# Slot tiles of the first expert layer: the h transposes ahead of the gathered rows' transpose on TensorE, with VectorE's two copies in the same order

## What is computed

```python
def _ffn(xn, rw, W1, W2):
    ms = jnp.mean(xn * xn, axis=-1, keepdims=True)
    h = xn * jax.lax.rsqrt(ms + RMS_EPS) * rw
    return jax.nn.silu(h @ W1) @ W2
...
gates = jax.nn.softmax(xf @ router_w, axis=-1)
top_v, top_i = jax.lax.top_k(gates, TOP_K)            # 2 of 14 experts
masked = jnp.zeros_like(gates).at[jnp.arange(N)[:, None], top_i].set(top_v)
masked = masked / (masked.sum(axis=-1, keepdims=True) + EPS)
routed_out = jnp.einsum('end,ne->nd', routed, masked)
return (routed_out + shared).reshape(B, T, D)         # 2 shared experts
```

## Time and profile before

| | us |
|---|---|
| runs of the kernel before | 988.82, 993.49, 994.43 (median 993.49) |
| the profiled execution, its own time | 996.92 |
| its span, first to last instruction | 995.2 |
| the slot loop in it: tile 0's gathered rows transposed to tile 44's output written | 367.1 to 445.7 |
| 40 of the 45 passes, first weight load of `slot_up` to the same 40 passes on | 377.35 to 441.56, 64.21 |

### The profile page before, as it was taken

How to read it: one execution, slowest core, us unless ns; L and a number is a source line. 1 busy time by engine, 2 the same in 40 slices (tenths; PEclk the granted TensorE clock), 3 DMA queues, 4 the chain that set the end, 5 groups by cost and what they waited for, 6 DMA issues and landing times.

```text
span 995.2 us, 18013 instructions
## 1 busy us (share of the span) xinstructions
PE 909.1 (91%) x5365; PEld 740.8 (74%) x5365; DVE 802.6 (81%) x2079; ACT 559.3 (56%) x1323; POOL 414.7 (42%) x480
## 2 busy tenths in 40 slices
PE   5999999999997898998878788988999999999995
PEld 5788888888884656765767676886667888888884
DVE  3778887888788955732898999986879999999996
ACT  2666666666667453444686433526775556655565
POOL 3566767576765425536540676642640000000001
PEclk7999999999998799999997999999999999999998
DMA  7232323333224103341102112001045666566651
GB/s 267 70 120 89 113 92 110 96 101 105 95 95 170 42 17 77 82 68 40 33 13 86 60 70 86 1 1 64 1 96 170 176 177 174 174 174 174 174 158 42
DMA packets 47122, 98.29 MB, mean 99 GB/s; under 512 B 7121, under 2 KB 23441, under 8 KB 45922
## 3 DMA queue, kind: packets, MB, share of 16 engines
q1 hardware_dynamic: 44610, 92.64, 30.2%
q0 software_dynamic: 2464, 5.05, 2.6%
HBM read 75.25 MB, written 22.41 MB: 98 GB/s over the span
## 4 chain that ended last, share of the span: by engine, by line
PE 66%; DVE 16%; issue 7%; ACT 5%; POOL 2%; DMA 1%; SPq 1%; another core or an unknown queue 0%; DVEq 0%; ACTq 0%; POOLq 0%
PE PS L1898 14%; PE PS L1899 13%; PE PS L1900 13%; PE PS L1965 4%; PE PS L1953 4%; PE PS L2144 3%; DVE rb L1695 2%; PE PS L1977 2%; PE PS L2158 2%; DVE P L1265 2%; PE PS L2087 1%; ACT P L903 1%; DVE keep L1676 1%; DVE xl L1235 1%; PE PS L2093 1%
## 5 line engine op out<-in xcount | busy, mean ns | idle before, releaser
L690 POOL TENSOR_TENSOR P<-P,rl 128x256 f32<-128x256 f32 (+1 forms) x130 | 104.9, 828 | 100.1 <-DVE rl L1272 100.1
L455 POOL TENSOR_TENSOR rs<-ms,neghalf 128x4 f32<-128x4 f32 (+1 forms) x28 | 26.0, 927 | 277.0 <-DVE nm L449 276.9
L1181 ACT ACTIVATE FG<-PS 128x512 f32<-128x512 f32 x112 | 67.1, 599 | 89.4 <-PE PS L1900 89.4
L903 ACT ACTIVATE P<-P,mn 128x128 f32<-128x128 f32 (+1 forms) x260 | 114.4, 444 | 3.1 <-DVE mn L1265 3.1
L1898 PE MATMUL PS<-XTh,W 128*128 128x512 f32 x256 | 100.5, 393 | 1.3 <-DMA W<-w3s 0.4
L1900 PE MATMUL PS<-XTh,W 128*128 128x512 f32 x256 | 99.7, 390 | 0.0
L1899 PE MATMUL PS<-XTl,W 128*128 128x512 f32 x256 | 99.7, 389 | 0.0
L1265 DVE CUSTOM_DVE_ANT_0 P<-PS,cmask 128x128 f32<-128x128 f32 (+1 forms) x260 | 77.1, 352 | 26.6 <-issue 26.6
L1864 DVE TENSOR_TENSOR FHL<-FH,FHH 128x512 fp32r<-128x512 f32 x128 | 90.0, 703 | 1.2 <-ACT FHH L1167 0.9
L1881 DVE TENSOR_TENSOR FU<-FG,PS 128x512 f32<-128x512 f32 x112 | 77.0, 687 | 16.1 <-ACT FG L1181 7.8
L911 ACT ACTIVATE Uh<-PS 128x512 fp32r<-128x512 f32 x64 | 38.4, 599 | 87.4 <-PE PS L1900 87.4
(11 more groups left out here) (479 smaller groups left out, 2609.2 us busy)
## 6 DMA issues: line engine op xcount, KB each, us to landing
GI<-coef SPq DMA_DIRECT2D x56, 256.0 KB, 4.2
GW<-coef SPq DMA_DIRECT2D x56, 256.0 KB, 4.1
w3s<-WS SPq DMA_DIRECT2D x32, 384.0 KB, 2.6
W<-w3s SPq DMA_DIRECT2D x32, 384.0 KB, 3.4
Wb<-decay SPq DMA_DIRECT2D x7, 1024.0 KB, 4.5
WR<-in_w SPq DMA_DIRECT2D x32, 192.0 KB, 2.5
WR<-in_w SPq DMA_DIRECT2D x16, 256.0 KB, 2.8
w12f<-WS SPq DMA_DIRECT2D x16, 256.0 KB, 2.0
```

Source lines behind the costliest of these rows:

```text
L690: last = pool.tensor_tensor(v, v, f, ALU.mult)
L903: last = act.activation(P[:, slot, c:c + w], P[:, slot, c:c + w], ACT.Exp, scale=-1.0, bias=mn[:, par, q:q + 1], accum_out=ls[:, par, q:q ...
L1181: act.activation(FG[:, k % 2, :], bank(4 + k % 2), ACT.Silu).then_inc(sem("fg_done"), 1)
```

## The change

On PE, `hidden_T(i-2)` is issued before `gather_T(i)` instead of after it. On DVE, the copy of `hTs` (with its waits) is issued before the copy of `xTs` (with its waits). No instruction is added or taken away, and no semaphore, buffer or shape changes. In the changed file the `hTs` copy has line 1533 and the `xTs` copy line 1538.

```diff
             for i in range(NT + 2):
+                if i >= 2:
+                    dve.wait_ge(sem("ht_ready"), on("ht_ready", i - 1))
+                    if i >= 4:
+                        dve.wait_ge(sem("yt_ready"), on("yt_ready", i - 3))
+                    dve.tensor_copy(hTs[i % 2][:, :], slot_hT).then_inc(sem("ht_done"), 1)
                 if i < NT:
                     dve.wait_ge(sem("xt_ready"), on("xt_ready", i + 1))
                     if i >= 2:
                         dve.wait_ge(sem("hs_ready"), on("hs_ready", i - 1))
                     dve.tensor_copy(xTs[i % 2][:, :], slot_xT).then_inc(sem("xt_done"), 1)
-                if i >= 2:
-                    dve.wait_ge(sem("ht_ready"), on("ht_ready", i - 1))
-                    if i >= 4:
-                        dve.wait_ge(sem("yt_ready"), on("yt_ready", i - 3))
-                    dve.tensor_copy(hTs[i % 2][:, :], slot_hT).then_inc(sem("ht_done"), 1)
...
             for i in range(NT + 3):
                 if 1 <= i < NT + 1:
                     slot_up(i - 1, experts[i - 1])
+                if 2 <= i < NT + 2:
+                    hidden_T(i - 2)
                 if i < NT:
                     gather_T(i)
-                if 2 <= i < NT + 2:
-                    hidden_T(i - 2)
```

## The result

| | before | changed |
|---|---|---|
| median of 8 runs, us | 993.22 (988.82 to 994.43) | 997.33 (996.9 to 1000.37) |
| 40 passes of the slot loop, us | 64.21 | 68.30 |
| one pass, median (shortest to longest), us | 1.54 (1.46 to 2.56) | 1.704 (1.70 to 1.80) |
| profiled execution, own time and span, us | 996.92, 995.2 | 997.02, 995.3 |

The changed kernel takes 1.0056 times as long, interval 1.0039 to 1.0073: slower by 4.1 us in the medians, where +5.0 was forecast. This ratio, like the others here, goes by the means of the runs (998.20 against 992.63, 5.6 us apart), and so it is a little larger than that of the medians. The 40 passes take 4.09 us more, where 4.2 was forecast.

A forecast was written before the change was run, and what follows sets the result against it. The prediction took PE's sequencer and matmuls to bound the slot loop, passing to a PE, VectorE, PE ring. Its terms 4.2 + 0.6 + 0.2 = +5.0 us took 993.5 to 998.5 us, range 993.0 to 1004.0.

The forecast's parts named there:

- The ring: Slot loop: PE, VectorE, PE hand-overs set the pace, 0.95 + 0.34 + 0.29 + 0.13 = 1.71 us a pass.
- T + 0.95, T + 1.29, T + 1.58: Slot loop, from `slot_up`'s weight load at T: `hTs` copy starts, `xTs` copy starts, `xTs` copy ends.
- Rival 4: VectorE in the slot loop: next copy waits for the previous one's end, 0.08 a pass, +3.4 us; chance 0.08.
- Rivals 1 to 3: Slot loop: `xTs` ready in time, 0 to 2 us, chance 0.2; a gain, 991.3, 0.05; late results compounding, 1002.5, 0.11.
- The cover: Slot loop: `xTs` is ready before PE's sequencer has its register, pass stays 1.55 to 1.60; chance 0.2.
- Late results: Slot loop: matmul results seen late, no longer paid for by slack, add 0.6 us, ends 0 and 2.
- a pass is set by PE's sequencer and matmuls: Slot loop before the change: other engines' results are ready earlier; a pass takes 1.605 us, 1.55 undisturbed.
- the wait is for the write of `Y` four tiles back: Two long passes before the change: `slot_down` waits for `Y`; the slower pace uses up most of this idle time.
- +4.2: Slot loop: 40 passes of 1.71 give 68.4 us against 64.2.
- First passes: Start of the slot loop: a pass of 1.35 becomes 1.71; counted as 0.2 us, ends 0 and 1.
- The stages before and behind the loop keep their lengths: Outside the slot loop: stage lengths unchanged, so a later loop end is passed on whole.
- PE's own row of work is as long as before.: PE in the slot loop: same matmuls and sequencer steps, so PE alone would keep its pass of 1.55.

The follow-up runs named there:

- e5: Changed kernel with two banks each for `slot_hT` and `slot_y`, no `ht_done` or `xt_done` waits on PE, looser `yt_done`: 1001.25 us, ratio 1.0056.
- e8: Changed kernel with only 128 of 256 columns of the `hTs` copy, output not the reference's: 991.06 us once, median pass 1.572.
- e3: Kernel before with only VectorE's copy order changed, TensorE's order kept: 1001.48 us, ratio 1.0134.
- e4: Kernel before without the redundant `xt_done` wait in `gather_T`: 987.97 us, ratio 0.9995.
- e7: Kernel before, own order kept, with the edits of e5: 993.28 us, ratio 0.9975.
- e10: Kernel before with eight `Y` buffers instead of four and nothing else: 994.15 us, ratio 0.9991.
- e9: e7 with eight `Y` buffers instead of four: 994.27 us, ratio 0.9991.
- e12: e9 without the gathers of tiles 4 to 44, output not the reference's: 980.46 us once, beside 992.0 for the kernel before.
- e11: Changed kernel run once more, no further edit: 998.7 us, ratio 1.0035.
- e2: Kernel before with only TensorE's order changed, VectorE's copy order kept: 993.02 us, ratio 1.0043.
- e6: The edit of e2 plus two `slot_hT` banks, `hidden_T` waiting for the copy of two tiles back: 994.37 us, ratio 0.9993.
- e1: Kernel before run again with a profile, no edit: 988.51 us, ratio 1.0001.

## Why the prediction was right, and where it wasn't

- **The ring.** T + 0.95, T + 1.29, T + 1.58 and a pass of 1.71 were forecast; 0.95, 1.29, 1.57 and 1.70 are in the trace. e5 shows that the waits for `Y` and for emptied banks don't hold the loop, e8 that the copy ahead counts fully, e3 that the same terms give 1.81 in the other order of transposes. The terms were read from single rows and added without averages: two hand-overs at which the receiving engine stood idle, VectorE's own distance from one copy to the next, and the length of a copy.
- **Rival 4**, the second copy behind the end of the first, is out: 403.53 is 0.08 before the end of a copy that started at 403.19 and took 0.42. The Trainium skill, page "VectorE: DVE Perf Modes", section "The DRAIN you can't avoid", says that the next operation waits until the pipe has emptied, but it goes on: "A next op that is not held starts earlier". The prediction took the first half alone for a disagreement. The start-to-start distances here, 0.34 behind a copy of 0.42 and in e8 0.21 behind one of 0.29, agree with the exception.
- **Rivals 1 to 3.** The cover doesn't hold: the pass is 1.70 and the copy ends 0.13 before the load. `hTs` comes earlier, with no gain. Late results didn't add up.
- **What bounded the loop before**, step "a pass is set by PE's sequencer and matmuls": half right. One wait less on the sequencer gave only 0.7 us in 40 passes (e4), and the pass fell to 1.35 when `slot_y`, `slot_hT` and their waits were given room too (e7). The forecast needed only that this pace is below 1.71.
- **The long passes**, step "the wait is for the write of `Y` four tiles back": wrong. The row itself says otherwise: ACT's idle time ahead of the late `Y` ends with `slot_down` (`1.44 <-PE PS L2158` in the earlier trace rows), not with a write. With eight buffers such passes remain (e10, e9), and without the gathers they are gone (e12). That they vanish in the changed kernel was forecast for the wrong reason, and to this extent the +4.2 was luck: it counts 2.4 us of the 64.2 as gone. What the runs show is only that none occurred in the 40 passes of the four traces with a steady pass of 1.70 or more (changed, e3, e5, e11).
- **Late results**, +0.6: none was seen in the 40 passes. **First passes**, +0.2: tile 4 is reached at 376.57 instead of 377.35, 0.8 earlier. The pass of 1.35 did become 1.70 as forecast, but it doesn't decide there: from tile 0's `slot_up` to tile 4's, e9 takes 8.44 us and e12, the same without the later gathers, 6.80, so the gathers hold the start in part. Both terms together were forecast at +0.8 and are -0.8, so that the loop ends 3.3 us later and not 5.0.
- **The profiled execution** was forecast at 1001.9 and took 997.02. Of the 4.9 us between, 1.7 are the loop's end just named and 2.2 the long VectorE operation in the trace of before; the rest isn't traced to a row. "The stages before and behind the loop keep their lengths" doesn't hold for single executions: behind the last `slot_down`, the traces from the chip of e5 to e12 differ by 3.6 us.
- **"PE's own row of work is as long as before."** True of the instructions, not of the waits. Moving `hidden_T` forward brings its wait for `ht_done` forward too, and alone costs 0.43% (e2, e6). The prediction treated both moves together and so needed no price for this; the expectation of e2 needed one, and was missed.
- **The base.** I took 64.2 us for the loop before. It is 61.8 without late results, so the steady cost is 6.5 us and not 4.1. In the median it is 4.1, and 3.9 in e11. That fits a loop of before that usually loses 2 us or more to late results where these medians were taken (64.21 before, 64.01 in e10). But those are only two traces, and there is none of the changed kernel from the chip of e1.

## What to carry over

In a pipelined loop over several engines, look for each closed ring of hand-overs and add up its start-to-start distances; the longest ring sets the pace, and PE's busy share doesn't show it (58.74 of 68.30 us here). Before a copy is put ahead of another, ask which of the two results is needed first by the engine that bounds the loop: here `xTs` is due in the next pass's first instruction, `hTs` only at its end. And a transpose that is moved takes its waits with it, which then stand ahead of everything queued on that engine's sequencer.

## What the runs showed of the hardware that was not expected

- Matmul results can be seen late at all other engines at once: by 0.3 to 1.4 us, about every third pass, at a pace of 1.35 (e7, e9); in some passes (before, e10) or in none of 40 (e1) at 1.54; in none of 40 at 1.70 or more, though in one of the first passes (changed, e5, e11); and in none without the gathers (e12). The matmul rows of the trace don't show it; their ends are modelled. It has to be read from the consumers.
- PE's sequencer is a resource of its own: the register load takes 0.30 us and the next step 0.15 in each of 40 passes, and a wait that is let go late delays the load behind it (e2: from 0.63 to 0.67 into the pass to 0.83).
- A VectorE operation of 0.16 us took 2.38 or 2.39 in three of 14 traces, one instruction of 28 in each, and each time as long as a GpSimd operation on large tiles that started 0.02 to 0.03 later. In the changed kernel's trace the same pair overlaps by 0.14 without this, so the overlap alone isn't the cause. It cost the profiled execution of before 2.2 us.
